# Cross-attention and feed-forward layer on one core: time rows paired before the forward transform, K and Q transformed in eight 64x32 tiles, a float32 inverse transform, and squares for the second layer norm taken by ScalarE

## The chip, the cores and the metric

One core of one Trainium2 chip. The metric is device time in microseconds (us) of one execution. The kernel before takes 1065.87 us, the median of 3 runs (1065.73 to 1066.18).

## What is computed

The input `x` holds 128 sequences of 128 rows (times) by 256 channels, and `ctx_1024` has the same shape. The reference, cut to what matters here:

```python
def reference(x, ctx, wq, wk, wv, wo, W_in, b_in, W_out, b_out):
    q = layernorm(x) @ wq;  k = ctx @ wk;  v = ctx @ wv      # 16 heads of 16
    corr = irfft(rfft(q, time) * conj(rfft(k, time)), n=128) # per channel
    top_vals, top_idx = top_k(corr, 4);  w = softmax(top_vals)
    out = sum_i w[i] * roll(v, top_idx[i] % 16, within the head)
    x = x + out @ wo
    h = quantize_a16(gelu(quantize_a16(layernorm(x)) @ quantize_w8(W_in) + b_in))
    return x + h @ quantize_w8(W_out) + b_out
```

## The kernel before, in words

The work has three stages. The attention stage takes the sequences in 64 pairs and runs them through a software pipeline: step t starts pair t and finishes pairs that were started up to six steps ago. The second stage multiplies the normalized rows by `W_in` (L635), and the third multiplies the quantized hidden values by `W_out` (L666). The change touches the attention stage alone, apart from one scale factor.

Every engine has its own instruction list in program order, and semaphores join them. The order in a list is written by hand: `step(t)` calls the functions of a step, `for t in range(PAIRS - 1)` repeats it, and the last pairs follow as a list of single calls. An engine never passes an instruction that waits.

**TensorE** (`step`, L575) does for pair t the products with `wk` (`project_k`, L464), with `wv` (`project_v`, L515), for pair t-4 with `wo` (`project_out`, L539), for pair t with `wq` (`project_q`, L477), for pair t-3 the weighting of V (`attend`, L527), for pair t the forward transforms of K and Q (`dft_k`, L489, and `dft_q`, L501), and for pair t-1 the inverse transform (`inverse`, L556). The products run in float16 with each operand cut into a high and a low part (three matmuls). The forward transforms are float32, with 128 rows and 64 columns of the array per matmul. The inverse is float16 in three parts, 64 rows by 128 columns. `project_k` and `project_q` write the same bank of PSUM (`bank[1]`), so each waits until the other's result has been taken.

**ScalarE** (`step`, L811) does, in this order: `spread_blocks` of pair t-4 (four copies of 32 partitions each, L756), `take_k` of t-1 (bank 1 to `kf`, through L686), `take_v` of t-1 (L730), `normalize2` of t-6 (second layer norm, L762), `high_ct` of t (high part of the context, L686), `high_cs` of t-2 (high part of the spectrum's product, L686), `exponent` of t-3 (L706), `take_q_scaled` of t-1 (bank 1 times the first layer norm's scale to `qf`, L718), `high_ot`, `high_xt`, `take_ot`, `take_q` (L746 and L747), and in some steps a piece of the weights' quantization.

**VectorE** (`step`, L1309) does: `weigh_hot` of t-4 (L1191), `moments2` of t-6 (L1268), `invert_sum`, `sum_hot`, `mask_sum`, `moments1` of t-1, `spread_weights` of t-4 (L1215), `top_values` of t-3 (four MAX8 on the correlation, L1291), `turn_weights` of t-4 (L1222), `products` of t-2 (L1230 and L1231), `top_places` of t-3, `head_lags`, `statistics1` of t (L1165), `one_hot` of t-3 (L1179), `magnitude` of t-6 (L1274), `residual` of t-5 (L1238), `sum_ex` of t-3, `statistics2` of t-5 (L1245), and in steps 10 to 31 a piece of the weights' scales (L1104, L1109).

**GpSimd** (`step`, L1021) does: `low_ct`, `low_cs` (L1002), `low_xt`, `low_ot` (low parts of the float16 splits), `scale_both` (the reciprocal roots of both layer norms), `add_terms` (L998) and `take_shift`. **SyncE** issues the loads and stores; the load of the next context pair waits for `low_ct` of the one before.

Two waits matter for what follows. `spread_blocks` waits for the transpose of the same pair:

```python
act.wait_ge(S["bt_done"], p + 1)      # in spread_blocks; set by turn_weights (VectorE)
```

and `take_q_scaled`, which frees the transform of Q, runs on ScalarE and waits for nothing of VectorE in its own step except the layer norm's scale.

Of the kernel before, what the change touches and what calls it, by code (L numbers as in the profile page):

```python
# [16 lines left out]
P = 128  # L17
# [4 lines left out]
UNROLL = 10  # L22
# [12 lines left out]
AHEAD = 5  # L35
# [9 lines left out]
C_ALL = C_ROW + 6  # L45
# [8 lines left out]
def by_head(a, axis):  # L54

    s = a.shape
    return a.reshape(s[:axis] + (HD, NH) + s[axis + 1:]).swapaxes(axis, axis + 1).reshape(s)


def constants():  # L60
# [5 lines left out]
    time = t % HD * NH + t // HD  # L66
    angle = 2 * np.pi * np.outer(t, f) / P
    table[:, C_DFT:C_DFT + NF] = np.cos(angle)
    table[:, C_DFT + NF:C_DFT + P] = -np.sin(angle)
    alternating = np.cos(np.pi * t)  # L70
    table[:, C_DFT] = 1 + alternating
    table[:, C_DFT + NF] = 1 - alternating
# [3 lines left out]
    sin[0] = -(1 - alternating) / (4 * P)  # L76
    inverse = np.zeros((P, 2, P))
    for n, m in enumerate((cos, -sin)):
        for b in range(2):
            inverse[b * NF:(b + 1) * NF, n, :] = m * G_UP  # L80
    inv16 = np.zeros((P, 2, 2, P), np.float16)
    inv16[:, 0] = inverse
    inv16[:, 1] = inverse - inv16[:, 0]
    table[:, C_DFT:C_DFT + P] = table[time, C_DFT:C_DFT + P]
# [3 lines left out]
    table[:, C_TURN] = np.where(t % NF == 0, Q_DOWN, -Q_DOWN)  # L88
    for k in range(9):
# [3 lines left out]
    return table.astype(np.float32), inv16  # L93


def xattn_ffn_kernel(nc, x, x_turned, ctx_turned, wq, wk, wv, wo, w_in, b_in, w_out, b_out, table, inv_table, out, x1_dram, h_dram):
# [4 lines left out]
    B, L, D = x.shape  # L101
# [7 lines left out]
    x_v = x.rearrange("(n b) l d -> n l b d", b=2)  # L109
# [4 lines left out]
    with ExitStack() as ctx:  # L114
# [12 lines left out]
        inv16 = sb("inv16", [P, 2, 2, P], F16)  # L127
# [38 lines left out]
        def cut(n, words, shape):  # L166
# [13 lines left out]
        cs16 = cut(1, 512, HALVES)[0].bitcast(F16).rearrange("p s (k e) -> p s k e", k=2)  # L180
# [6 lines left out]
        csum = prod[:, :, 0, :]  # L187
# [17 lines left out]
        half = cut(1, 4, BOTH)[0]  # L205

# [36 lines left out]
            ln2_stats v_done q_done vt_out q_out terms_done sums_done inv_done sc_top hd_done  # L243
            top_done shift_done exp_done mt_out ot_done ot_out ot_low sum_high cs_ready ct_high
# [3 lines left out]
            c_hi_dve c_lo c_f c_out first_int y_inverse bias_chain bias_ready kp_done kf_out k_done w2_done  # L248
# [50 lines left out]
        def _(sp):  # L299
# [12 lines left out]
            def load_turned(p):  # L312
                wait(sp, S["ct_ready"], p)
                sp.dma_start(cturn, ctx_turned[p]).then_inc(s_t_in, 16)
# [14 lines left out]
            def step(t):  # L329
# [10 lines left out]
                if t == 1:  # L340
                    sp.dma_start(inv16[:, :, :, :], inv_table).then_inc(S["direct_in"], 16)
# [91 lines left out]
        def _(pe):  # L433
# [15 lines left out]
            def keep_warm(n, k, table_of=None):  # L449
# [1146 lines left out]
```

## Time and profile before

| what | value |
| --- | --- |
| median of 3 runs | 1065.87 us |
| span of the profiled execution, first to last instruction | 1064.2 us |
| attention stage, to the first matmul of the second stage | 595.2 us |
| TensorE, ScalarE, VectorE, GpSimd busy over the span | 98%, 88%, 91%, 47% |
| granted TensorE clock, mean of the span | 1.000 |

The profile gives no other time of its own execution than the span; 1.7 us of the median lie around it. An instruction's row gives its start and its duration. Neighbours on VectorE and ScalarE overlap by some 0.08 us, so what one of them costs its engine is the distance to the next start, not its duration. Durations in one row of several instructions are those of the merged stretch.

### The profile page before, as it was taken

How to read it: one execution, taken by the hardware profiler on the slowest of the kernel's cores; microseconds unless marked ns; L12 is line 12 of the kernel's file. 1: busy time of each engine (PE TensorE's matmuls, PEld its weight loads, DVE VectorE, ACT ScalarE, POOL GpSimd, SP SyncE). 2: the span in 40 equal slices, each digit the busy share in tenths (PEclk: the TensorE clock that was granted, in tenths of full speed). 3: DMA queues.
4: the chain of work that ended last, by engine and by line, in shares of the span. 5: the costliest groups of instructions: out<-in, count | busy, mean ns of one | idle time of the engine just before them, and what ended most of it. 6: DMA issues, size and time to landing. Idle time of an engine off the chain costs nothing.

```text
span 1064.2 us, 28999 instructions
## 1 busy us (share of the span) xinstructions
PE 1047.4 (98%) x9358; PEld 778.0 (73%) x9358; DVE 965.1 (91%) x2768; ACT 939.9 (88%) x1697; POOL 505.0 (47%) x674
## 2 busy tenths in 40 slices
PE   8999999999999999999998899999999999999998
PEld 6788888888888888888887444444444888888887
DVE  4789999999988888888889999999997999999998
ACT  5888888899999998888888688888888999999996
POOL 5788888888888888888887400000001000000000
PEclk9999999999999999999999999999999999999999
DMA  5454444334445443444431498999999999999995
GB/s 178 130 150 145 121 121 120 121 120 120 121 120 140 121 120 120 121 120 120 120 111 41 132 325 301 300 305 316 309 300 342 356 347 363 355 354 355 346 364 195
DMA packets 141665, 222.59 MB, mean 209 GB/s; under 512 B 72432, under 2 KB 92272, under 8 KB 137456
## 3 DMA queue, kind: packets, MB, share of 16 engines
q1 hardware_dynamic: 140464, 220.12, 62.8%
q8 instruction: 61, 1.00, 0.4%
q10 hardware_dynamic: 1088, 1.05, 0.3%
q14 instruction: 52, 0.43, 0.1%
HBM read 121.00 MB, written 83.89 MB: 193 GB/s over the span
## 4 chain that ended last, share of the span: by engine, by line
PE 94%; ACT 2%; DVE 2%; issue 1%; DMA 1%; POOL 0%; ACTq 0%; DVEq 0%; POOLq 0%
PE sums L666 21%; PE bank L635 10%; PE sums L635 10%; PE sums L464 8%; PE sums L477 8%; PE bank L515 8%; PE sums L539 7%; PE sums L489 6%; PE bank L527 5%; PE bank L501 5%; PE bank L556 5%; PE sums L672 1%; DMA store_x<-in_L_xattn_wv 1%; ACT arena L756 0%; ACT arena L686 0%
## 5 line engine op out<-in xcount | busy, mean ns | idle before, releaser
L666 PE MATMUL sums<-wout,arena 128*128 128x256 f16 x2048 | 229.8, 273 | 1.2 <-DVE arena L1521 1.2
L666 PEld LDWEIGHTS sums<-wout,arena 128*128 128x128 f16 x2048 | 196.9, 98 | 32.5 <-DVE arena L1514 7.3
L1521 DVE SCALAR_TENSOR_TENSOR arena<-arena,wout_rel 128x512 f16<-128x512 int16 x256 | 180.3, 746 | 2.0 <-ACT arena L935 0.9
L756 ACT ACTIVATE arena<-arena 32x128 f32<-32x128 f32 x256 | 78.6, 307 | 47.8 <-DVE arena L1222 45.5
L635 PE MATMUL sums<-arena,win 128*128 128x512 f16 x512 | 115.9, 379 | 1.0 <-DVE arena L1466 0.9
L635 PE MATMUL bank<-arena,win 128*128 128x512 f16 x512 | 115.7, 379 | 0.0
L686 ACT ACTIVATE arena<-arena 128x512 f16<-128x512 f32 x192 | 112.9, 617 | 1.6 <-POOL arena L998 1.1
L1485 DVE TENSOR_REDUCE hmax_all<-arena 128x1 f32<-128x1024 f32 x96 | 111.3, 1211 | 2.9 <-ACT arena L892 2.9
L935 ACT ACTIVATE arena<-arena,wout_rel 128x512 f16<-128x512 int16 x159 | 106.2, 706 | 0.0
L892 ACT ACTIVATE arena<-sums,b_in_sb,z_scale 128x512 f32<-128x512 f32 x128 | 97.4, 778 | 9.8 <-PE sums L635 4.9
L1088 POOL CAST store_x<-one 128x1 bf16<-128x1 f32 x1 | 0.2, 189 | 220.0 <-DVE one L1503 220.0
L928 ACT ACTIVATE arena<-arena,one 128x1536 int16<-128x1536 f32 x63 | 99.2, 1575 | 4.5 <-DVE arena L1521 3.0
L1010 POOL TENSOR_TENSOR arena<-arena 128x512 f16<-128x512 f32 x64 | 74.2, 1159 | 54.8 <-ACT arena L686 54.8
L1291 DVE MAX8 arena<-bank 128x8 f32<-128x128 f32 x256 | 57.1, 286 | 46.9 <-PE bank L556 46.8
L477 PE MATMUL sums<-store_x,arena 128*128 128x256 f16 x768 | 94.3, 273 | 1.0 <-ACT arena L686 0.5
L515 PE MATMUL bank<-arena,store_x 128*128 128x256 f16 x768 | 94.3, 273 | 1.0 <-ACT arena L686 0.6
L635 PEld LDWEIGHTS sums<-arena,win 128*128 128x128 f16 x512 | 50.0, 98 | 61.9 <-issue 1.4
L464 PE MATMUL sums<-store_x,arena 128*128 128x256 f16 x768 | 95.0, 273 | 0.0
L635 PEld LDWEIGHTS bank<-arena,win 128*128 128x128 f16 x512 | 50.1, 98 | 60.4
L539 PE MATMUL sums<-store_x,arena 128*128 128x256 f16 x762 | 93.7, 273 | 0.4 <-POOL arena L1006 0.4
L998 POOL TENSOR_TENSOR arena<-arena 128x512 f32<-128x512 f32 x64 | 81.4, 1272 | 3.5 <-DVE arena L1231 3.4
L477 PEld LDWEIGHTS sums<-store_x,arena 128*128 128x128 f16 x768 | 74.9, 98 | 10.4 <-issue 0.8
(141 smaller groups left out, 2303.7 us busy)
## 6 DMA issues: line engine op xcount, KB each, us to landing
hidden_scratch<-arena SPq DMA_DIRECT2D x32, 1536.0 KB, 5.5
arena<-hidden_scratch SPq DMA_DIRECT2D x64, 768.0 KB, 6.7
arena<-in_ctx_turned SPq DMA_DIRECT2D x64, 256.0 KB, 2.6
arena<-in_x_turned SPq DMA_DIRECT2D x64, 256.0 KB, 2.9
arena<-in_x SPq DMA_DIRECT2D x64, 256.0 KB, 3.7
x_scratch<-arena SPq DMA_DIRECT2D x64, 256.0 KB, 3.4
arena<-x_scratch SPq DMA_DIRECT2D x32, 512.0 KB, 6.0
out<-arena SPq DMA_DIRECT2D x31, 512.0 KB, 4.2
```

Source lines behind the costliest of these rows:

```text
L464: last = nc.tensor.matmul(bank[1][:, b * D:(b + 1) * D], ct16[:, i, c, b * P:(b + 1) * P], w16[:, j, 3, c, :], start=c == 0 and k == 0, st ...
L477: last = nc.tensor.matmul(bank[1][:, b * D:(b + 1) * D], xt16[:, i, c, b * P:(b + 1) * P], w16[:, j, 0, c, :], start=c == 0 and k == 0, st ...
L515: last = nc.tensor.matmul(bank[7][:, e * D:(e + 1) * D], w16[:, j, 1, c, e * P:(e + 1) * P], ct16[:, i, c, :], start=c == 0 and k == 0, st ...
L539: last = nc.tensor.matmul(pair(7)[:, 1, :] if p == PAIRS - 1 and b == 1 else pair(0)[:, b, :], ot16[p % 2][:, i, c, b, :], w16[:, j, 2, c, :],
L635: last = nc.tensor.matmul(bank[f][:, :].rearrange("p (n t) -> p n t", n=4), win16[:, f, c, :], xt[q % 3][:, s, :, c, :], start=s == 0 and ...
L666: last = nc.tensor.matmul(bank[m * 2 + k // 2][:, k % 2 * D:(k % 2 + 1) * D], gbuf[:, s, f, k * P:(k + 1) * P], wout16[:, f, :], start=f = ...
L686: nc.scalar.activation(dst, src, ACT.Copy).then_inc(S[done], 1)
L892: nc.scalar.activation(dst, bank[b][:, :], ACT.Gelu, bias=b_in_sb[:, f:f + 1], scale=z_scale[:, f:f + 1]).then_inc(S[done], 1)
L928: nc.scalar.activation(hq[:, a:b, :].rearrange("p f t -> p (f t)"), src, ACT.Copy, scale=h_up).then_inc(S["c_hq"], 1)
L935: nc.scalar.activation(gbuf[:, 0, f, :], hq[:, f, :], ACT.Copy, scale=wout_rel[:, f:f + 1]).then_inc(S["c_hi_act"], 1)
L1485: V.tensor_reduce(hmax[:, bass.ds(q, 1), k], halls[m][:, 2 * k:2 * k + 2, :], AX_XY, ALU.max, apply_absolute_value=True).then_inc(S["b_max ...
L1521: V.scalar_tensor_tensor(gbuf[:, 1, f, :], hq[:, f, :], wout_rel[:, f:f + 1], gbuf[:, 0, f, :], ALU.mult, ALU.subtract).then_inc(S["c_lo"], 1)
```

## The change

- Host layout: rows t and t+64 of a pair are placed side by side (the inputs are permuted; for the context, the order within the pair is turned around).
- `mix_ct` (new, GpSimd): sum and difference of the context's two halves, before the float16 split. `high_ct` waits for it, and so does the next load of the context.
- `take_q_half` (ScalarE) takes half of Q from the bank with its scale; `mix_q` (new, VectorE) makes the sum and the difference from the bank's other half. They take the place of `take_q_scaled`.
- `transform` takes the place of `dft_k` and `dft_q`: 16 float32 matmuls of 64 rows by 32 columns.
- `inverse` becomes 8 float32 matmuls; `high_cs` and `low_cs` go.
- TensorE's order: `project_q` comes before `project_out`.
- Second layer norm, all but the last five pairs: `residual` in two halves that also give sums, `minus_mean2` (GpSimd), `squares` (ScalarE); `statistics2` and `moments2` go. `normalize2` and `magnitude` move one step later.
- `wo` is loaded in four DMAs and mixed on VectorE once.

```diff
-UNROLL = 10
+UNROLL = 8
-AHEAD = 5
+AHEAD = 6
+BY_BN = 5
+XN_UP = 16.0
...
-            def dft_k(p):
+            def transform(p):
                 if p == 0:
                     pe.wait_ge(S["const_in"], 16)
                 pe.wait_ge(S["kf_out"], p + 1)
                 wait(pe, S["terms_done"], p)
-                for r in range(2):
-                    for b in range(2):
-                        last = nc.tensor.matmul(bank[3][b * NF:(b + 1) * NF, r * D:(r + 1) * D], dft[:, r * NF:(r + 1) * NF], kf[:, b, :],
...
                 pe.wait_ge(S["qf_out"], p + 1)
                 wait(pe, S["q_out"], p)
                 for r in range(2):
+                    for src, dst, turned in ((kf, 3, 1), (qf, 4, 0)):
+                        for b in range(2):
+                            rows = slice((b ^ turned) * NF, (b ^ turned) * NF + NF)
+                            for odd in range(2):
+                                strip = slice((b * 2 + odd) * 32, (b * 2 + odd) * 32 + 32)
+                                last = nc.tensor.matmul(bank[dst][strip, r * D:(r + 1) * D], dft[rows, odd * NF + r * 32:odd * NF + r * 32 + 32], src[rows, odd, :],
+                                                        start=True, stop=True)
+                last.then_inc(S["kq_done"], 1)
...
-                pe.wait_ge(S["cs_ready"], p + 1)
+                pe.wait_ge(S["sums_done"], p + 1)
...
+                        for b in range(2):
+                            half_of = slice(b * NF, (b + 1) * NF)
+                            last = nc.tensor.matmul(bank[5 + b][:, e * P:(e + 1) * P], csum[half_of, k, e * P:(e + 1) * P],
+                                                    inv32[half_of, k, :], start=k == 0, stop=k == 1)
...
             def step(t):                      # TensorE
                 if active(t, 0):
                     project_k(t)
                     project_v(t)
+                    project_q(t)
                 if active(t, 4):
                     project_out(t - 4)
-                if active(t, 0):
-                    project_q(t)
...
-            def take_q_scaled(p):
+            def take_q_half(p):
                 act.wait_ge(S["qp_done"], p + 1)
                 act.wait_ge(S["scales_done"], p + 1)
+                wait(act, S["qf_out"], p)
+                nc.scalar.activation(q_half, pair(1)[:, 1, :], ACT.Copy, scale=rs[(p + AHEAD) % 2][:, 1, 1, :]).then_inc(S["q_half_out"], 1)
...
+            def squares(p):
+                act.wait_ge(S["nm_done"], p + 1)
+                for b in range(2):
+                    last = nc.scalar.activation(xnt[:, p, b, :], x1[p % 2][:, b, :], ACT.Square, bias=nm[p % 2][:, b, :], scale=1.0, accum_out=mv[p % 2][:, 0, b, 1:2])
+                last.then_inc(S["ln2_stats"], 1)
...
-                if active(t, 6):
-                    normalize2(t - 6)
+                if active(t, 7):
+                    normalize2(t - 7)
...
-                if active(t, 2):
-                    high_cs(t - 2)
                 if active(t, 3):
                     exponent(t - 3)
                 if active(t, 1):
-                    take_q_scaled(t - 1)
+                    take_q_half(t - 1)
+                if active(t, 6):
+                    squares(t - 6)
+                if active(t, 0):
+                    high_xt(t)
...
+            def mix_ct(p):
+                pool.wait_ge(s_t_in, p * 16 + 16)
+                wait(pool, S["ct_high"], p)
+                wait(pool, S["ct_ready"], p)
+                nc.gpsimd.tensor_tensor(sd[:, :, 0:P], cturn[:, :, 0:P], cturn[:, :, P:2 * P], ALU.add)
+                nc.gpsimd.tensor_tensor(sd[:, :, P:2 * P], cturn[:, :, 0:P], cturn[:, :, P:2 * P], ALU.subtract).then_inc(S["ct_mixed"], 1)
...
+            def mix_q(p):
+                dve.wait_ge(S["q_half_out"], p + 1)
+                wait(dve, S["kq_done"], p)
+                for k, op in enumerate((ALU.add, ALU.subtract)):
+                    last = V.scalar_tensor_tensor(qf[:, k, :], pair(1)[:, 0, :], rs[(p + AHEAD) % 2][:, 1, 0, :], q_half, ALU.mult, op)
+                last.then_inc(S["qf_out"], 1)
...
+                for b in range(2):            # residual, all but the last five pairs
+                    last = V.scalar_tensor_tensor(x1[p % 2][:, b, :], pair(0)[:, b, :], 1.0 / W_UP, xin[p % UNROLL][:, b, :], ALU.mult, ALU.add,
+                                                  accum_out=mv[p % 2][:, 0, b, 0:1])
+                last.then_inc(S["x1_done"], 1)
...
                 if active(t, 3):
                     top_places(t - 3)
                     head_lags(t - 3)
+                if active(t, 1):
+                    mix_q(t - 1)
                 if active(t, 0):
                     statistics1(t)
                 if active(t, 3):
                     one_hot(t - 3)
-                if active(t, 6):
-                    magnitude(t - 6)
+                if active(t, 7):
+                    magnitude(t - 7)
```

## Rows read from the trace of the kernel before

**Rows 1.** The page: its head and its first part, busy us by engine.

```profile
span 1064.2 us, 28999 instructions
PE 1047.4 (98%) x9358; PEld 778.0 (73%) x9358; DVE 965.1 (91%) x2768; ACT 939.9 (88%) x1697; POOL 505.0 (47%) x674
```

**Rows 2.** Busy us of each engine over twenty steps; then clock, DMA share, GB/s.

```profile
227.80:405.50 177.70, 177.70 (x1921) 146.18 (x1920) 160.33 (x666) 162.96 (x381) 153.14 (x201) 1.00 0.42 122
```

**Rows 3.** Timeline of TensorE over one step: start, us, engine, line, operation.

```profile
305.13 1.48 PE L464 MATMUL sums<-store_x,arena 128*128 128x256 f16 x12
...
307.76 1.47 PE L539 MATMUL sums<-store_x,arena 128*128 128x256 f16 x12
...
310.38 1.06 PE L527 MATMUL bank<-arena,store_x 128*128 128x128 f32 x8
311.37 1.08 PE L489 MATMUL sums<-arena,cst 128*64 128x256 f32 x8
...
313.25 0.84 PE L556 MATMUL bank<-inv,arena 64*128 64x128 f16 x24
314.02 0.28 PE L464 MATMUL sums<-store_x,arena 128*128 128x256 f16 x1
```

**Rows 4.** Timeline of VectorE over the same step.

```profile
305.24 0.89 DVE L1291 MAX8 arena<-bank 128x8 f32<-128x128 f32 x4 [0.85 <-PE bank L556]
306.05 0.29 DVE L1222 STREAM_TRANSPOSE arena<-arena 128x128 f32<-128x128 f32 x1
...
308.71 0.74 DVE L1165 BATCH_NORM_STATS2 arena<-arena 128x6 f32<-128x256 f32 x2
309.37 0.41 DVE L1179 TENSOR_TENSOR sums<-cst,sums 128x256 f32<-128x256 f32 x1
309.90 0.69 DVE L1274 TENSOR_REDUCE xmax<-store_x 128x1 f32<-128x512 f32 x1
310.50 0.68 DVE L1238 SCALAR_TENSOR_TENSOR arena<-sums,arena 128x512 f32<-128x512 f32 x1
...
311.22 0.75 DVE L1245 BATCH_NORM_STATS2 arena<-arena 128x6 f32<-128x256 f32 x2
311.89 0.42 DVE L1191 TENSOR_TENSOR sums<-sums,arena 128x256 f32<-128x256 f32 x1
312.21 0.24 DVE L1268 BATCH_NORM_AGGREGATE arena<-arena 128x2 f32<-128x6 f32 x2
...
313.00 0.29 DVE L1215 TENSOR_TENSOR arena<-arena,sums 128x128 f32<-128x128 f32 x1
```

**Rows 5.** Timeline of ScalarE over the same step.

```profile
306.38 1.26 ACT L756 ACTIVATE arena<-arena 32x128 f32<-32x128 f32 x4 [0.55 <-DVE arena L1222]
307.66 0.60 ACT L686 ACTIVATE arena<-sums 128x512 f32<-128x512 f32 x1
308.16 0.59 ACT L730 ACTIVATE store_x<-bank 128x512 f32<-128x512 f32 x1
308.78 1.09 ACT L762 ACTIVATE store_x<-arena 128x256 f32<-128x256 f32 x2
309.78 1.13 ACT L686 ACTIVATE arena<-arena 128x512 f16<-128x512 f32 x2
...
310.92 0.81 ACT L718 ACTIVATE arena<-sums,arena 128x256 f32<-128x256 f32 x2
```

**Rows 6.** Groups by line and shape: count, busy us, mean ns, idle before and releaser.

```profile
L1254 DVE SCALAR_TENSOR_TENSOR arena<-sums,arena 128x256 f32<-128x256 f32 x1 | 0.4, 425 | 0.0
L1078 POOL TENSOR_TENSOR store_x<-b_out_sb,store_x 128x256 f32<-128x256 f32 x1 | 0.7, 671 | 0.1
L1002 POOL TENSOR_TENSOR arena<-arena 128x512 f16<-128x512 f32 x64 | 74.1, 1158 | 2.4 <-ACT arena L686 2.4
L1104 DVE TENSOR_REDUCE win_max<-store_x 128x1 f32<-128x256 f32 x8 | 3.2, 402 | 0.0
L1109 DVE TENSOR_SCALAR win_max<-win_max 128x8 f32<-128x8 f32 x1 | 0.9, 881 | 0.0
```

More of the change, by code:

```diff
@@ L79, in constants @@
         for b in range(2):
[L80 to L84, printed above, removed]
+            inverse[b * NF:(b + 1) * NF, n, :] = m[by_parity] * G_UP
     table[:, C_ID:C_ID + P] = np.eye(P)
@@ L847, in _ @@
             take_k(PAIRS - 2)
-            normalize2(PAIRS - 7)
+            normalize2(PAIRS - 8)
             exponent(PAIRS - 4)
             high_ct(PAIRS - 1)
+            take_v(PAIRS - 2)
+            take_q_half(PAIRS - 2)
+            squares(PAIRS - 7)
             high_xt(PAIRS - 1)
-            take_q_scaled(PAIRS - 2)
-            high_cs(PAIRS - 3)
-            take_v(PAIRS - 2)
             take_q(PAIRS - 2)
@@ L857, in _ @@
             spread_blocks(PAIRS - 5)
+            take_q_half(PAIRS - 1)
             exponent(PAIRS - 3)
-            take_q_scaled(PAIRS - 1)
+            normalize2(PAIRS - 7)
             high_ot(PAIRS - 5)
-            high_cs(PAIRS - 2)
             take_ot(PAIRS - 5)
             take_q(PAIRS - 1)
+            squares(PAIRS - 6)
             spread_blocks(PAIRS - 4)
             high_ot(PAIRS - 4)
-            high_cs(PAIRS - 1)
             take_ot(PAIRS - 4)
@@ L1023, in step @@
                     low_ct(t - 1)
-                if active(t, 3):
-                    low_cs(t - 3)
+                if active(t, 0) and t > 0:
+                    mix_ct(t)
                 if active(t, 1):
@@ L1038, in _ @@
             low_ct(PAIRS - 2)
-            low_cs(PAIRS - 4)
+            mix_ct(PAIRS - 1)
             low_xt(PAIRS - 2)
-            scale_both(PAIRS - 7)
+            minus_mean2(PAIRS - 7)
+            scale_both(PAIRS - 8)
             take_shift(PAIRS - 4)
@@ L1362, in _ @@
             top_places(PAIRS - 4)
-            magnitude(PAIRS - 7)
+            mix_q(PAIRS - 2)
+            magnitude(PAIRS - 8)
             sum_ex(PAIRS - 4)
@@ L1370, in _ @@
             residual(PAIRS - 6)
-            statistics2(PAIRS - 6)
             invert_sum(PAIRS - 4)
             weigh_hot(PAIRS - 4)
-            moments2(PAIRS - 6)
             sum_hot(PAIRS - 4)
+            top_values(PAIRS - 3)
+            mix_q(PAIRS - 1)
             products(PAIRS - 2)
-            top_values(PAIRS - 3)
             top_places(PAIRS - 3)
```

200 lines of the change are left out of this document (99 added, 101 removed).

## The prediction

> **What bounds the kernel now.** I read the page first: over the whole span TensorE is busy 98%, ScalarE 88%, VectorE 91% [rows 1]. A share over three stages says little about one of them, so I took twenty steps out of the middle of the attention stage: TensorE is busy 177.70 of 177.70 us, which is 8.89 us a step, at a granted clock of 1.00; per step VectorE has 8.02 us of work, ScalarE 8.15 (a few weight pieces among it), GpSimd 7.66 [rows 2]. TensorE sets the pace, and the others have less than 1.3 us a step to spare. The reader should see both: shortening TensorE's list pays at once, and it can't pay much before another engine, or a chain through several, takes over.
>
> Then one step in order of time. On TensorE it runs from 305.13 to 314.02: `project_k` and `project_v` take 2.63 us, the attend 0.99, the two forward transforms 1.88 and the inverse 0.77 [rows 3]. On VectorE the one long idle stretch, 0.85 us, lies ahead of the MAX8, which waits for the inverse; the transpose that follows it ends 0.04 us before ScalarE's four copies start, and those had waited 0.55 us for it [rows 4, 5]. So VectorE and ScalarE are led by TensorE once a step. Today nothing on VectorE waits for ScalarE's later half of the same step, so no circle closes without TensorE.
>
> **TensorE, part by part.** The forward transforms are 8 float32 matmuls of 256 columns in 1.88 us, two side by side (K and Q of either sequence in 64 columns of the array each), with a change of tile shape at the end [rows 3]. That is 0.47 us per pair of matmuls. The new ones are 16 of the same 256 columns, and eight different tiles can run at once. If they do, two rounds cost 4/8 of the streaming now, 0.9 us, and about 0.1 for the change of shape: 1.0. The bounds are 1.0 from below and, if only two run together, twice today's, 3.8; half concurrency gives 1.9. I take 1.0, because two tiles already share the array without loss.
>
> The inverse was 24 float16 matmuls in 0.77 us. Now it is 8 in float32 of 128 columns. The attend has 4 float32 matmuls of 128 columns and full size in 0.99 us [rows 3]; eight half-size ones, two side by side, are the same streaming, so 0.99; if they don't overlap, 1.98. I take 0.99. Together TensorE's list falls from 8.89 to 8.89 - 1.88 - 0.77 + 1.0 + 0.99 = 8.23 us. Moving `project_q` ahead of `project_out` costs TensorE no time of its own, but leaves `take_k` only `project_v` as cover (1.31 us) where it had two products (2.63).
>
> **GpSimd** loses `low_cs` (1.16) and gains `mix_ct`, two float32 additions of 256 columns at 0.67 each (1.34), and `minus_mean2`, a small operation I put at 0.25 [rows 6]: 7.66 + 0.43 = 8.1 us. It stays under what follows. `mix_ct` now releases the context's load, earlier than `low_ct` did, so SyncE's queue is not late.
>
> **ScalarE** loses `high_cs` (0.52) and one of the two halves of `take_q_scaled` (0.36) and gains two squares, at the 0.5 us that `normalize2` takes per half [rows 5] plus a sum's read-out, which no row shows; between 0 and 0.2 each, 0.1 taken. Net +0.3, 8.5 us a step with weight pieces, under 10.
>
> **VectorE** loses `statistics2` (311.22 to 311.89, 0.67) and `moments2` (0.24 less 0.08 of overlap, 0.16). It gains `mix_q`, two operations like L1254's 0.425, so 0.34 apart with the overlap and 0.65 to 0.70 for both [rows 6]. `residual` was 0.60 (0.68 less 0.08) and becomes two halves at 0.34 with a sum each; the sum's read-out has no row, bounds 0 and 0.15 each, 0.05 taken: 0.78. In all 8.02 - 0.67 - 0.16 - 0.60 + 0.65 + 0.78 = 8.0 us.
>
> By sums of work alone, then, every engine would fit in 8.2 to 8.5 us, and the step would shrink. But **the change adds a wait on VectorE**, and I have to name what is queued behind it. `mix_q` of pair t-1 waits for `take_q_half` of pair t-1, which is the seventh call in ScalarE's step. The first call of that same ScalarE step, `spread_blocks`, waits for `turn_weights` of the same VectorE step. And VectorE reaches the next `turn_weights` only after `mix_q` and all that stands behind it. That is a circle of one step, without TensorE in it, and its length is a floor for the step:
>
> - ScalarE, from the first copy to `take_q_scaled`: 306.38 to 310.92, 4.54 us. Out of it go `high_cs` (half of 1.13 for two overlapped copies, 0.52) and the 0.12 that `normalize2` now waits (308.16 + 0.49 to 308.78) [rows 5]. Left 3.90, plus `take_q_half` to its end, 0.45: **4.35**.
> - VectorE, from the place of `mix_q` (just ahead of L1165, 308.71) to L1215 at 313.00: 4.29, plus 0.21 for L1215 itself. Out go 0.67, 0.16, and the 0.20 that L1274 waits (309.37 + 0.33 to 309.90). Left 3.47. MAX8 to transpose 0.81, transpose 0.29 [rows 4]: 4.57. In come `mix_q` 0.65 and 0.18 more for `residual`: **5.40**.
> - Two crossings at the 0.04 us seen between transpose and copies: 0.09.
>
> Sum 9.84 us. VectorE then works 8.0 us and stands 1.8 ahead of `mix_q` in each step. TensorE, with 8.2 us of work, waits for `take_k` (queued behind the copies) ahead of `project_q`.
>
> At this point a page helps to place it. The Trainium skill, TensorEngine Tiling (Array Packing), section PSUM Bottleneck, says that packing speeds up TensorE but not the taking of its results, which may then become the bottleneck. By that rule the change can't keep what its tiles save; by TensorE's sum alone it would.
>
> **The sum.** Full circles run from step 7, where `magnitude` and `normalize2` begin, to about step 61: 54 steps of +0.95, **+51 us**. VectorE's weight pieces stood in its idle time; now they lie on the circle: sixteen of L1104 at 0.402 less 0.08 are 5.1, and six or so short ones, of which the four like L1109 (0.88, 0.80 apart) make up 3.2, come to some 3.7 [rows 6], **+9**. ScalarE's pieces come after `take_q`, in time that it still has: nothing. Filling: `mix_ct` of pair 0 comes ahead of the first split (1.3), and steps 1 to 6 have shorter circles, near 8.2 to 9: **+1.5**. The last pairs: two more `mix_q` round trips and one more small operation of GpSimd for each of the last five, against the shorter inverse chain: **+3**. The second and third stages keep their instructions. Total +64. The profiled execution would go from 1064.2 to 1128, and the median, 1.7 above its span, from 1065.9 to **1130**. The unknown sizes move it so: each 0.1 us on the circle is 5.5 us. `residual`'s sums at 0 give -5, at 0.15 each +11; `mix_q` at 0.80 gives +8. Its own range is 1120 to 1145.
>
> **Rivals.**
>
> *The tiles pay (ends faster).* If ScalarE and VectorE were not held to one another, TensorE's list would be the step: 8.23, 60 steps of -0.66, with +3 for filling and emptying 1066 - 40 + 3 = 1029. For it: the 98% of TensorE, and that no engine has more than 8.5 us of work. Against it: the circle, which needs only that both lists run in order. It decides where the circle is under 8.9, so 0.95 us would have to be missing from it, of which no term but `mix_q` and `residual` is unmeasured. 6%.
>
> *The tiles don't run together.* At 1.9 for the transforms the list is 9.1 and still hidden: about +7 from the first steps, 1137. With 1.98 for the inverse as well it is 10.1, and because MAX8 waits for the inverse and `project_q` for `take_k`, the circle through TensorE (MAX8 0.81, transpose 0.33, copies 1.29, `take_k` 0.60, then `project_q`, `project_out`, attend, transforms, inverse: 7.5) is 10.6 us, some 1174. With two tiles at a time (3.8) it goes beyond 1220. For it: no row shows more than two tiles at once, and each of the eight streams its own data. Against it: two side by side cost nothing. The same page's section Tiling Modes lists 64x32 as eight independent tiles, which is why I don't give this more. 10%.
>
> *The circle is partly cut.* The order of events may let `take_q_half` start earlier than I add up, for example if some of what I counted in series overlaps: a step near 9.3, 1080 to 1115. The step before closes in my terms to 0.05 us, which speaks against it. 6%.
>
> **Chances.** Forecast 78%, tiles partly or not together 10%, partly cut 6%, faster 6%. The range 1110 to 1160 leaves out the fast case and the worst packing. A measurement of this kernel tells 0.2%, 2 us, from no change: faster 0.06, same 0.01, slower 0.93.
>
> **What would show it.** In the changed profile: a step of 9.8 us in the middle of the attention stage; VectorE idle about 1.8 us ahead of `mix_q`, released by ScalarE's copy; MAX8 no longer waiting for the inverse; ScalarE waiting near 2 us for the transpose; TensorE idle about 1.5 us, ahead of `project_q` first of all; the transforms in 1.0 us and the inverse in 1.0. If VectorE's idle time stands ahead of MAX8 again and the step is 8.2 to 8.4, the circle isn't there and I am wrong. If the transform takes over 1.9 us, the packing failed. Steps with weight pieces should be longer by the piece.

## The result, and the profile after

The changed kernel takes **1144.86 us** (median of 4 runs, 1143.14 to 1146.68), the kernel before beside it 1065.8 us. The ratio is **1.0743**, 95% interval 1.0728 to 1.0758: slower by 7.4%, or 79 us. The profiled execution has a span of 1143.1 us, 1.8 under the median; TensorE's granted clock is 0.998 over the span, where it was 1.000; one stretch of the filling is behind that, and it is looked at further below.

The page of the changed kernel, head and first part, answers to [rows 1]:

```profile
span 1143.1 us, 30275 instructions
PE 1024.5 (90%) x9870; PEld 759.9 (66%) x9870; DVE 970.0 (85%) x2838; ACT 942.9 (82%) x1805; POOL 518.1 (45%) x742
```

All busy times hardly moved (TensorE 23 us less, VectorE, ScalarE and GpSimd 3 to 13 us more), but the shares fell. The kernel hasn't more work to do, it waits more. The same stretch as in [rows 2], and one step of it (columns as there):

```profile
227.80:405.50 177.70, 147.89 (x1794) 121.66 (x1792) 140.01 (x602) 144.37 (x367) 135.61 (x191) 1.00 0.35 111
350.28:360.31 10.03, 8.53 (x107) 7.01 (x105) 7.90 (x36) 8.22 (x21) 7.83 (x12) 1.00 0.34 108
```

No engine has more than 8.53 us of work in a step of 10.03 us. Who waits for whom is in the waits of that stretch (engine, line that waited, what ended the wait: us in total, times, longest):

```profile
DVE arena L1250 <- ACT arena L716: 35.5, 17, 2.1
...
ACT arena L748 <- DVE arena L1243: 32.7, 18, 2.0
PE sums L477 <- ACT arena L677: 29.8, 18, 1.8
POOL arena L1021 <- ACT arena L677: 27.3, 17, 1.6
```

L1250 is `mix_q`, L716 `take_q_half`, L748 the four copies of `spread_blocks`, L1243 `turn_weights`. VectorE waits for ScalarE once a step, ScalarE for VectorE once a step, and both for about as long: that is what a circle of two in-order lists looks like. TensorE and GpSimd each wait for ScalarE once a step (GpSimd also 7.7 us in all for VectorE), and nobody waits for them. The timelines of one step; VectorE first, against [rows 4]:

```profile
350.28 0.88 DVE L1326 MAX8 arena<-bank 128x8 f32<-128x128 f32 x4
351.08 0.29 DVE L1243 STREAM_TRANSPOSE arena<-arena 128x128 f32<-128x128 f32 x1
...
355.91 0.88 DVE L1250 SCALAR_TENSOR_TENSOR arena<-sums,arena 128x256 f32<-128x256 f32 x2 [2.09 <-ACT arena L716]
356.71 0.74 DVE L1186 BATCH_NORM_STATS2 arena<-arena 128x6 f32<-128x256 f32 x2
...
358.28 0.42 DVE L1271 SCALAR_TENSOR_TENSOR arena<-sums,arena 128x256 f32<-128x256 f32 x1
358.62 0.08 DVE L1271 DVE_READ_ACCUMULATOR arena<-sums,arena 128x1 f32 x1
358.62 0.42 DVE L1271 SCALAR_TENSOR_TENSOR arena<-sums,arena 128x256 f32<-128x256 f32 x1
...
360.31 0.88 DVE L1326 MAX8 arena<-bank 128x8 f32<-128x128 f32 x4
```

ScalarE, against [rows 5]:

```profile
351.40 1.26 ACT L748 ACTIVATE arena<-arena 32x128 f32<-32x128 f32 x4 [1.69 <-DVE arena L1243]
352.69 0.60 ACT L677 ACTIVATE arena<-sums 128x512 f32<-128x512 f32 x1
353.19 0.59 ACT L722 ACTIVATE store_x<-bank 128x512 f32<-128x512 f32 x1
353.80 1.09 ACT L760 ACTIVATE store_x<-arena 128x256 f32<-128x256 f32 x2
...
355.43 0.45 ACT L716 ACTIVATE arena<-sums,arena 128x256 f32<-128x256 f32 x1
355.79 0.49 ACT L754 ACTIVATE store_x<-arena 128x256 f32<-128x256 f32 x1
356.19 0.19 ACT L754 ACTIVATION_READ_ACCUMULATOR store_x<-arena 128x1 f32 x1
356.28 0.49 ACT L754 ACTIVATE store_x<-arena 128x256 f32<-128x256 f32 x1
```

TensorE, against [rows 3] (the transforms' first and last lines; four pairs of such lines follow one another every 0.2 us):

```profile
353.43 1.47 PE L477 MATMUL sums<-store_x,arena 128*128 128x256 f16 x12 [1.50 <-ACT arena L677]
...
356.05 1.06 PE L521 MATMUL bank<-arena,store_x 128*128 128x128 f32 x8
357.04 0.42 PE L495 MATMUL sums<-arena,cst 64*32 64x256 f32 x4
...
357.74 0.40 PE L495 MATMUL bank<-arena,cst 64*32 64x256 f32 x4
358.07 1.16 PE L550 MATMUL bank<-inv,arena 64*128 64x128 f32 x16
359.17 1.48 PE L464 MATMUL sums<-store_x,arena 128*128 128x256 f16 x12
```

The sixteen transform matmuls take 357.04 to 358.07, 1.03 us, where the eight of the kernel before took 1.88: the eight tiles do run together. TensorE's gain is there, and more than it is lost again ahead of `project_q`, 1.50 us.

Where the 79 us arise is read from the start of `project_k` of some pairs, and of the second stage, in the timelines of TensorE (us):

| | pair 7 | pair 10 | pair 33 | pair 50 | pair 61 | stage 2 |
|---|---|---|---|---|---|---|
| before | 65.0 | 91.7 | 296.2 | 447.4 | 545.2 | 595.2 |
| after | 71.7 | 101.8 | 339.1 | 509.6 | 620.3 | 674.2 |

Filling to pair 7: +6.7. Pairs 7 to 61: +68.4, of which weight pieces 6.6 (pairs 10 to 33 take 237.3 us, 23 steps of 10.03 would be 230.7). The last pairs: +3.9. From there to the end it is 468.9 us against 469.0: stages 2 and 3 are unchanged.

### The profile page after: what moved, and what is told of

It is laid out like the page before. It is cut to its first block and busy times, and to the rows that moved or that the text cites. A ratio compares the mean times of both kernels' runs of the same rounds, so it can differ in the third digit from the quotient of the medians.

```text
span 1143.1 us, 30275 instructions
## 1 busy us (share of the span) xinstructions
PE 1024.5 (90%) x9870; PEld 759.9 (66%) x9870; DVE 970.0 (85%) x2838; ACT 942.9 (82%) x1805; POOL 518.1 (45%) x742
## 5 line engine op out<-in xcount | busy, mean ns | idle before, releaser
L748 ACT ACTIVATE arena<-arena 32x128 f32<-32x128 f32 x256 | 78.5, 307 | 118.5 <-DVE arena L1243 116.2
L1250 DVE SCALAR_TENSOR_TENSOR arena<-sums,arena 128x256 f32<-128x256 f32 x128 | 56.1, 480 | 130.5 <-ACT arena L716 130.5
L477 PEld LDWEIGHTS sums<-store_x,arena 128*128 128x128 f16 x768 | 70.7, 97 | 116.8 <-issue 108.9
L1021 POOL TENSOR_TENSOR arena<-arena 128x512 f16<-128x512 f32 x64 | 74.3, 1160 | 94.6 <-ACT arena L677 94.6
L534 PE MATMUL sums<-store_x,arena 128*128 128x256 f16 x762 | 93.6, 273 | 0.4 <-POOL arena L1017 0.4
L626 PEld LDWEIGHTS sums<-arena,win 128*128 128x128 f16 x512 | 49.9, 98 | 61.6 <-issue 1.2
L509 PEld LDWEIGHTS bank<-arena,store_x 128*128 128x128 f16 x768 | 75.0, 98 | 10.6 <-DVE store_x L1147 1.6
```

What stands on the lines that cost most here:

```text
L477: last = nc.tensor.matmul(bank[1][:, b * D:(b + 1) * D], xt16[:, i, c, b * P:(b + 1) * P], w16[:, j, 0, c, :], start=c == 0 and k == 0, st ...
L509: last = nc.tensor.matmul(bank[7][:, e * D:(e + 1) * D], w16[:, j, 1, c, e * P:(e + 1) * P], ct16[:, i, c, :].rearrange("p (s b j) -> p b ...
L534: last = nc.tensor.matmul(pair(7)[:, 1, :] if p == PAIRS - 1 and b == 1 else pair(0)[:, b, :], ot16[p % 2][:, i, c, b, :], w16[:, j, 2, c, :],
L626: last = nc.tensor.matmul(bank[f][:, :].rearrange("p (n t) -> p n t", n=4), win16[:, f, c, :], xt[q % 3][:, s, :, c, :], start=s == 0 and ...
```

## The experiments

Theory A: the circle of the prediction, with `mix_q` as its closing link, sets the step. All kernels are the changed one with the edit shown. `us` is the device time; "step" is pair 33 to pair 50 over 17, in which no weight piece falls. The kernel before, on the same chips, gave 1066.24, 1065.89, 1065.65 and 1065.8. e7 and e9 to e12 are medians of four or five runs, the others one run each. The device times carry a few us of TensorE's clock: in every trace but those of e5 and of the kernel before there are one to three stretches, 3.4 to 10.2 us each, in the filling or the last pairs, in which the granted clock was 0.50. No stretch of that kind lies between pair 33 and pair 50, so the steps are the surer measure.

| run | us | step | stage 2 starts |
|---|---|---|---|
| changed kernel | 1144.9 | 10.03 | 674.2 |
| e1 project_q after project_out | 1146.1 | 10.03 | 675.3 |
| e2 mix_q late | 1085.5 | 9.03 | 614.8 |
| e3 copy off the circle | 1149.8 | 10.04 | 678.4 |
| e4 copy on the circle | 1174.8 | 10.55 | 703.9 |
| e5 transpose ahead of MAX8 | 1106.4 | 9.37 | 635.6 |
| e6 e2 and e5 | 1075.4 | 8.87 | 604.7 |
| e7 three moves | 1070.4 | 8.75 | 599.6 |
| e8 immediate in mix_q | 1137.7 | 9.92 | 667.0 |
| e9 five moves | 1057.2 | 8.56 | 586.0 |
| e10 e9, wo by SyncE | 1056.5 | 8.53 | 585.8 |
| e11 six moves | **1044.8** | 8.36 | 573.8 |
| e12 e11, bn statistics | 1070.2 | 8.65 | 599.5 |

**e1: is it TensorE's new order?**

```diff
                     project_v(t)
-                    project_q(t)
                 if active(t, 4):
                     project_out(t - 4)
+                if active(t, 0):
+                    project_q(t)
```

> One edit to the changed kernel: TensorE's project_q goes back behind project_out. The changed kernel's step is 10.03 us in the middle of the attention stage and TensorE idles 1.50 us of it ahead of project_q, waiting for ScalarE's copy of K. Theory A (a circle through VectorE and ScalarE, from mix_q to the transpose and from the four copies to take_q_half): TensorE isn't in the circle, so the step stays at 10.0 and the time at 1145 within 3 us; the 1.5 us of idle time only move. Theory B (the reorder is the loss: the copy of K has 1.31 us of cover where it had 2.63): the wait shrinks by most of 1.3 us, the step falls to 8.8 to 9.2 and the time to 1080 to 1095.

1146.1 us, and the step moved by less than 0.01 us. The waits from 296 to 400 us show that TensorE only waits elsewhere now, ahead of the transforms (L495):

```profile
DVE arena L1251 <- ACT arena L717: 20.9, 10, 2.1
...
PE sums L495 <- DVE arena L1251: 12.6, 10, 1.3
```

An engine that is led can have its list put in another order for nothing. The order of TensorE is not the cause.

**e2: `mix_q` behind `magnitude`.** Three operations leave the circle (`statistics1`, `one_hot`, `magnitude`: 356.71 to 358.28 above, 1.57 us), with no work removed.

```diff
-                if active(t, 1):
-                    mix_q(t - 1)
                 if active(t, 0):
                     statistics1(t)
...
                     magnitude(t - 7)
+                if active(t, 1):
+                    mix_q(t - 1)
```

> One edit to the changed kernel: in VectorE's step mix_q moves from ahead of statistics1 to behind magnitude, that is behind 1.6 us of its own work (0.66 + 0.32 + 0.60). Theory A: VectorE did nothing for 2.09 us ahead of mix_q; with 1.6 us of work put there the circle through mix_q is broken up to the rest, and the next floor takes over, the circle through TensorE: MAX8 0.81, transpose 0.33, four copies 1.29, copy of K 0.64, project_q, project_out, attend 3.61, transforms 1.03, inverse 1.15, in all 8.9. Step 8.9 to 9.0, time 1070 to 1078. Theory B (reorder) and theory C (ScalarE's list has become too long by the squares): the order inside VectorE's step changes nothing, step 10.0, time 1145.

1085.5 us: 59 of the 79 us are gone by moving one call. The step, 9.03, is 0.03 above the range that I expected. The time is 7 to 15 us above mine, and that was my arithmetic: 57 steps that are 1.03 to 1.13 shorter take 1144.9 to between 1080 and 1086, not to 1070 to 1078. The step fell by 1.00 and not by the full 1.57 that left the circle, and the waits from 296 to 400 us tell why:

```profile
ACT arena L748 <- DVE arena L1243: 7.7, 12, 0.8
DVE arena L1326 <- PE bank L550: 5.7, 12, 0.6
PE sums L477 <- ACT arena L677: 5.4, 11, 0.5
```

MAX8 waits for the inverse again: a second circle, through TensorE, is the next floor. By the rows of the changed kernel: MAX8 to the copies 1.12, the copies 1.29, `take_k`'s start to `project_q` 0.74, `project_q` and `project_out` 2.62, the attend 0.99, transforms 1.03, inverse 1.10, and some 0.1 back to MAX8: 9.0.

**e3 and e4: the same extra work, off the circle and on it.** One ScalarE copy of 512 columns into a spare buffer, ahead of `squares` (e3) or ahead of the high part of the context (e4).

```diff
+                nc.scalar.activation(spare[:, :], x1[p % 2].rearrange("p b d -> p (b d)"), ACT.Copy)    # e3, in squares
...
+                nc.scalar.activation(spare[:, :], sd.rearrange("p c k -> p (c k)"), ACT.Copy)           # e4, in high_ct
```

> The changed kernel with one more ScalarE copy of 128x512 in each step, 0.52 us, at the start of squares, which is behind take_q_half; its result is not used. Theory A: that place is off the circle, and ScalarE stands idle 1.69 to 2.2 us a step ahead of the four copies, so the step stays 10.0 and the time 1145 within 4 us. Theory C (ScalarE's amount of work sets the pace): +0.52 us for each of some 58 steps, 1175.

> The changed kernel with the same extra copy of 128x512 on ScalarE, 0.52 us, but at the start of high_ct, which stands between the four copies and take_q_half. Theory A: this place is on the circle, so each step grows by all of it, 10.03 to 10.55, and the time by 0.52 x 57, about 30 us, to 1175 (1170 to 1180). Theory C gives the same here, so it is the pair with the run that has the copy off the circle that tells them apart. Theory B: ScalarE's idle time takes it, 1145 to 1150.

The steps are 10.04 and 10.55: nothing off the circle, the full 0.52 us on it. In device time +4.9 and +29.9 us. The 4.9 of e3, a little over the 4 that I allowed, aren't a price of the steps: 0.6 us of them are there at pair 7, 1.0 at pair 61, and 3.2 come between pair 61 and the second stage, where the granted clock was 0.50 for 6.8 us (649.6 to 656.4) as it wasn't in the changed kernel. An attend, a `project_out` and a `project_v` there take 6.65 us for 3.97 in the changed kernel. The last 0.7 lie outside the span. This pair is the sharpest proof of the circle: half a microsecond of the same work costs 0.52 us a step in one place and 0.01 in another place of the same list.

**e5 and e6: the transpose ahead of MAX8, alone and with e2.** `turn_weights` has its data before MAX8 starts, so it can go first, and ScalarE's copies with it.

```diff
-                if active(t, 3):
-                    top_values(t - 3)
                 if active(t, 4):
                     turn_weights(t - 4)
+                if active(t, 3):
+                    top_values(t - 3)
```

> One edit to the changed kernel: in VectorE's step turn_weights (the transpose) goes ahead of top_values (four MAX8, 0.80 us); mix_q stays where it is. Theory A: the circle from mix_q over the transpose to take_q_half loses exactly the MAX8: 10.03 - 0.80 = 9.23 us a step, over 57 steps 46 us less than 1145, that is 1097 to 1103. The four copies then no longer wait behind a MAX8 that waits for the inverse. Were the wait ahead of MAX8 what counts (theory B's form of it, a circle through TensorE), nothing would be won, since no wait ahead of MAX8 is left in the changed kernel: 1145.

> Both edits of VectorE's order: the transpose ahead of MAX8 and mix_q behind magnitude. Theory A: with mix_q late the floor was the circle through TensorE (9.03 a step in that run, 0.8 of it the MAX8); taking MAX8 out of it leaves 8.2, below TensorE's own list of 8.37 (three products and project_out 5.24, attend 0.99, transforms 1.03, inverse 1.10) and near VectorE's 8.0 and GpSimd's 8.1. Step 8.4 to 8.7, 58 steps of -0.33 to -0.63 against the run with mix_q late (1085.5): 1049 to 1067. If some unseen load other than the two circles held the step at 9.0, no gain: 1085.

e5 gives 9.37 a step where the circle less MAX8's 0.80 would be 9.23, and 1106.4 us, 3 above the expectation. e6 shortens both circles and gives 8.87 and 1075.4 us, not the 8.4 to 8.7 and at most 1067 that their lengths promised: a miss, so there had to be a third.

**e7: `take_q_half` ahead of the exponent as well.**

```diff
+                if active(t, 1):
+                    take_q_half(t - 1)
                 if active(t, 3):
                     exponent(t - 3)
-                if active(t, 1):
-                    take_q_half(t - 1)
```

> The two edits of VectorE's order, and on ScalarE take_q_half one call earlier, ahead of exponent (0.11 us and its wait for GpSimd's take_shift). Theory A: it can only help if exponent's wait is on the path to mix_q: step 8.4 to 8.6, time 1045 to 1062, below the kernel before. If TensorE's list is reached already, the same time as with the two edits within 3 us.

1070.4 us, ratio to before 1.0052 (1.0036 to 1.0067), step 8.75. That is 5 us better than e6 and again short of what I expected (8.4 to 8.6 a step, at most 1062 us). Its waits from 296 to 400 us:

```profile
ACT store_x L722 <- PE bank L509: 4.5, 12, 0.5
PE sums L495 <- DVE arena L1250: 3.7, 12, 0.8
DVE arena L1250 <- ACT arena L716: 2.3, 12, 0.2
```

Read from top to bottom this is the third circle: ScalarE's `take_v` (L722) waits for `project_v`, `mix_q` waits for ScalarE, the transforms wait for `mix_q`. With the spacings of the rows it is `take_v` 0.62, normalizations 1.0, high copies 0.52, `take_q_half` 0.45, `mix_q` 0.88, transforms 1.03, inverse 1.10, `project_k` and `project_v` 2.62, and the hand-over from `mix_q`'s end to the transforms 0.25: 8.47. Two more hand-overs, 0.14 from `project_v` to `take_v` and 0.04 from `take_q_half` to `mix_q`, make it 8.65. The mean of 17 steps is 8.75.

**e8: the price of `mix_q`.** The second operand is a number in place of a scale per row, so this kernel leaves out the scale of one half of Q.

```diff
-V.scalar_tensor_tensor(qf[:, k, :], pair(1)[:, 0, :], rs[(p + AHEAD) % 2][:, 1, 0, :], q_half, ALU.mult, op)
+V.scalar_tensor_tensor(qf[:, k, :], pair(1)[:, 0, :], 1.0, q_half, ALU.mult, op)
```

> The changed kernel with mix_q's per-partition scale replaced by the number 1.0 (the scale of this half of Q is left out). In the changed kernel the two operations of mix_q start 0.40 us apart, and residual's, of the same size with a constant and a sum, 0.34. Theory: the scale read from memory is the 0.06 us. Then the circle loses 0.12 us, the step is 9.91 and the time 7 us less, 1138. If the 0.06 comes of something else (the operands' places), no change: 1145 within 3 us.

1137.7 us. The lines' own view, of the changed kernel and then of this one (ns: least, median, most):

```profile
L1250 DVE SCALAR_TENSOR_TENSOR arena<-sums,arena x128: 473/480/488, 16.0 to 642.7; 128x256 f32<-128x256 f32 x128
```

```profile
L1250 DVE SCALAR_TENSOR_TENSOR arena<-sums,arena x128: 414/420/426, 14.8 to 634.0; 128x256 f32<-128x256 f32 x128
```

A scale read from memory costs 0.06 us an operation, 0.12 a step on the circle, 7 us of device time.

**e9: V read later, GpSimd's scales earlier.** On top of e7:

```diff
                     take_k(t - 1)
-                    take_v(t - 1)
...
                     high_ct(t)
...
+                if active(t, 1):
+                    take_v(t - 1)
                 if active(t, 1):
                     take_q_half(t - 1)
...
-                if active(t, 5):
-                    low_ot(t - 5)
                 if active(t, 6):
                     minus_mean2(t - 6)
                 scale_both(t - 7)
+                if active(t, 5):
+                    low_ot(t - 5)
```

> All of the three moves before, and two more: ScalarE reads V out of PSUM (take_v) only after the first normalizations and the high parts of C, and GpSimd computes the scales of layer norm 2 (scale_both) ahead of the low parts of the weighted V. Nothing is left out. Theory A (what sets the step with three moves is a circle of 8.7 us: project_v's end, take_v 0.62, the normalizations 1.0, the high copies 0.52, take_q_half 0.45, mix_q 0.88, a crossing 0.25, the transforms 1.03, the inverse 1.10, then the projections of K and V): with take_v off it, the circle is 0.6 us shorter, and TensorE's own list, 8.3 to 8.4 us, takes over: pair 33 to pair 50 at 8.35 to 8.5 us a step against 8.74, stage 2 from about 580, device time 1048 to 1058 us. Rival C (the step of 8.74 us is VectorE's or ScalarE's own sum, and no order changes it): 1068 to 1072 us.

1057.2 us, ratio 0.9926 (0.9909 to 0.9943): the first version ahead of the kernel before, by 0.7%. The time is in my range, the step, 8.56, a little above it. The waits from 296 to 400 us, then one hand-over in the timeline of GpSimd and in that of SyncE's queue, name the reason:

```profile
POOL arena L1013 <- DMA arena<-in_ctx_turned: 7.6, 10, 1.9
...
PEld sums L534 <- POOL arena L1018: 2.8, 4, 1.1
```

```profile
338.31 1.16 POOL L1026 TENSOR_TENSOR arena<-arena 128x512 f16<-128x512 f32 x1
```

```profile
339.49 0.33 SPq L318 DMA_DIRECT2D arena<-in_x_turned  x1
...
340.82 0.48 SPq L314 DMA_DIRECT2D arena<-in_ctx_turned  x1
```

The context's buffer is free at 338.3, when `mix_ct` is done, but its load is the fourth in SyncE's queue, behind one that waits for `low_xt` (L1026) and two more. It is issued at 340.8, GpSimd starts late with it, and `project_out` (L534) waits for GpSimd.

**e10: is the filling slow by the load of wo?** In the changed kernel ScalarE's queue issues four transfers of wo for 2.69 us in the first step. Here SyncE issues them one step later, and what uses them follows.

```diff
 # SyncE, t == 1
+                    load_wo()
...
 # ScalarE
-                if t == 0:
-                    load_wo()
-                if t == 1:
+                if t == 2:
                     high_w(2)
...
 # VectorE
-                if t == 1:
+                if t == 2:
                     mix_wo()
                     low_w(2, 3)
```

> As the run before it, and the four transfers that bring wo in for its two halves are issued by SyncE one step later in place of ScalarE, with the mix of wo and its split a step later too. Nothing is left out. Theory A (the filling lost some 5 us of its 6.7 because these issues held 2.69 us of ScalarE's queue at 10.55 us, ahead of take_k of pair 0): pair 10 starts 3 to 5 us earlier than in the run before it, and so does everything behind; 1044 to 1054 us. Rival (the filling is slow since each first step is a circle of its own, and the issues only happened beside it): no change, within 1 us.

1056.5 us, within 1 us of e9, and pair 10 even starts 2.0 us later (99.1 against 97.1). By its number the rival holds: this move buys nothing. But the run doesn't clear the issues. TensorE's wait ahead of the first `project_q` fell from 2.54 to 0.77 us, as the theory wants, and yet the first transforms start only 0.47 us earlier (17.10 against 17.57). VectorE's timeline shows what else stands there once `mix_q` is late: it is behind `statistics1`, and that waits for the load of x of the next pair:

```profile
15.43 0.75 DVE L1186 BATCH_NORM_STATS2 arena<-arena 128x6 f32<-128x256 f32 x2 [2.82 <-DMA arena<-in_x]
...
25.36 0.75 DVE L1186 BATCH_NORM_STATS2 arena<-arena 128x6 f32<-128x256 f32 x2 [3.86 <-DMA arena<-in_x]
```

The first of these waits is in e9 too (4.07 us). The second is not: with the wo issues in SyncE's queue, the context's load behind them goes out at 16.12 in place of 12.76, and the next load of x at 22.44 in place of 20.26. The move took one wait away and made another. What the issues cost in the changed kernel, where `mix_q` stands ahead of `statistics1`, no run shows.

**e11: the context's load first.** On top of e9, in SyncE's step:

```diff
-                if active(t, 0) and t > 0:
+                if active(t, 0) and 0 < t <= 5:
                     load_turned(t)
+                if t >= 5:
+                    load_turned(t + 1)
                 if active(t, 0) and t > 0:
                     load_x_turned(t)
```

> The five moves before, and a sixth on SyncE's queue: from pair 5 on, the load of the transposed context rows of the next pair is issued as soon as GpSimd has mixed the last ones, ahead of the load of the transposed rows of x, which waits for their low parts. Nothing is left out. Theory D (with five moves GpSimd has become part of the circle: it waited 7.6 us in 104 for this transfer, which stood 1.3 us behind the end of the low parts in SyncE's queue, and TensorE's project_out then waited for the low parts of the weighted V, 4.3 us in the same stretch): both waits go or shrink, pair 33 to pair 50 at 8.36 to 8.48 us a step against 8.56, device time 1048 to 1054 us. Rival E (8.56 us is already TensorE's own list, 102 us busy in 104): within 1.5 us of 1057.2 us.

**1044.8 us** (1044.26 to 1045.47), ratio 0.9804 (0.9788 to 0.982), 3 us below my range. Six moves with no work removed turn 7.4% slower into 2.0% faster. Busy time of the engines from 296 to 400 us, and then the longest waits that are left there:

```profile
296.00:400.00 104.00, 104.00 (x1285) 87.90 (x1284) 99.87 (x425) 101.94 (x260) 97.23 (x138) 1.00 0.46 136
```

```profile
PEld bank L551 <- issue: 4.9, 12, 0.4
DVE arena L1328 <- PE bank L551: 3.3, 12, 0.3
...
```

TensorE is busy for all of the 104 us, and the step is its list again, 8.36 us in place of 8.89. This version beats both kernels.

**e12: what does the layer norm part bring there?** e11 with the second layer norm's sums taken back to `bn_stats` and `bn_aggr`:

```diff
-BY_BN = 5
+BY_BN = 64
...
 # ScalarE
-                    squares(t - 6)
...
 # GpSimd
-                    minus_mean2(t - 6)
...
 # VectorE
+                    moments2(t - 6)
...
+                    statistics2(t - 5)
```

> The kernel of the run before it, with the layer norm part of the change undone alone: the residual no longer sums its rows, ScalarE's squares and GpSimd's mean are gone, and VectorE computes the statistics of layer norm 2 with bn_stats and bn_aggr as before the change. Nothing is left out. Theory F (with its idle time gone VectorE is close to the limit, so the layer norm part carries its own weight): VectorE's list, some 8.1 us without its waits, gets 0.67 + 0.16 us longer and sets the step at 8.9 to 9.0 us, device time 1072 to 1082 us. Rival G (ScalarE is the closer one, 98.5 us busy in 104, and loses 1 us a step by this): no change or faster, at most 1 us above the run before it.

1070.2 us, 25.5 above e11. From 296 to 400 us:

```profile
296.00:400.00 104.00, 102.52 (x1252) 84.92 (x1251) 103.07 (x423) 90.10 (x206) 96.00 (x144) 1.00 0.44 129
```

VectorE is busy for 103.07 of 104 us: theory F. The step, 8.65, is below my 8.9, and the time 2 us below my range; but with VectorE full, its weight pieces cost too: pairs 10 to 33 take 208.9 us, 9.08 a step. Without this part of the change the faster transforms would bring nothing, even in the order of e11 (ratio to before 1.0043, 1.0026 to 1.0059).

## Why the prediction was right, and where its terms were off

The forecast was 1130 us with a range of 1110 to 1160 and 93% for slower; measured 1144.86. The mechanism stands: e2, e3 with e4, and e5 each move the step as a circle does, and e1 rules out TensorE's order. Of the 15 us by which the forecast is low, some 10 are the circle's length, 5 the filling, 1 the last pairs, and the weight pieces give 2 back. By its own steps:

- **The circle, 9.84 us.** Measured 10.03: ScalarE's part 4.48 for 4.35 (351.40 to 355.88), VectorE's 5.49 for 5.40, crossings 0.06 for 0.09. ScalarE's 0.13 is the 0.12 that I took out ahead of `normalize2` as a wait: it is there still (353.19 to 353.80 with nothing to wait for). On VectorE `mix_q` takes 0.80 to the next start, not 0.65, of which 0.12 are its scale's coming from memory (e8); L1254 [rows 6], which I priced it by, has 0.425. This outweighs `residual`, 0.69 for 0.78.
- **54 steps, +51 us.** It was +61.8 (68.4 less 6.6); 54 × 1.14 are 61.6. The 0.19 us of the circle makes the 10 us.
- **Weight pieces, +9.** 6.6, the steps of pairs 10 to 31 being 10.1 to 10.5 us long, as the forecast says that they should. The sixteen reductions cost what I gave them (0.33 to the next start, 5.2 in all). The seven short ones between 184 and 319 us cost 1.3 in all, not 3.7: the four that I priced at 0.80 by L1109 are 0.25 to 0.27 from their next one here, though their lines of the kernel are the same. Why they are shorter is open.
- **Filling, +1.5.** This is the term that was off by most for its size: +6.7. The 1.3 that I gave `mix_ct` isn't there at all: `project_k` of pair 0 starts at 7.22, before at 7.42. The steps that follow I had at 8.2 to 9, and from pair 1 on they are 8.6 to 9.1, but I set them against a full step of 8.89, and the kernel before fills faster than that: from pair 0 to pair 4 its steps are 7.25, 8.23, 7.14 and 8.29, where these are 10.88, 8.99, 8.92 and 8.61. TensorE's timeline of the first steps, then ScalarE's:

```profile
14.03 1.47 PE L477 MATMUL sums<-store_x,arena 128*128 128x256 f16 x12 [2.58 <-ACT arena L677]
17.07 0.42 PE L495 MATMUL sums<-arena,cst 64*32 64x256 f32 x4 [1.57 <-DVE arena L1250]
24.37 0.42 PE L495 MATMUL sums<-arena,cst 64*32 64x256 f32 x4 [1.96 <-DVE arena L1250]
33.88 0.42 PE L495 MATMUL sums<-arena,cst 64*32 64x256 f32 x4 [1.68 <-DVE arena L1250]
...
42.49 0.42 PE L495 MATMUL sums<-arena,cst 64*32 64x256 f32 x4 [0.78 <-DVE arena L1250]
```

```profile
10.55 2.69 ACTq L690 DMA_DIRECT2D store_x<-in_L_xattn_wo  x4
13.29 0.60 ACT L677 ACTIVATE arena<-sums 128x512 f32<-128x512 f32 x1 [2.11 <-issue]
```

  In the kernel before, the longest wait ahead of the transform of Q in these pairs is this one, in pair 1:

```profile
21.11 1.08 PE L501 MATMUL bank<-arena,cst 128*64 128x256 f32 x8 [1.32 <-ACT arena L718]
```

  Three things are in these rows. In the first three pairs nothing stands between `project_q` and the transforms, in the fourth only the attend, to cover the way through ScalarE and now VectorE too: 6.0 us of waits ahead of L495, where the kernel before had 1.55 ahead of its transform of Q. `project_q` of pair 0 waits 2.58 us for `take_k`, where before it waited 0.50, and ScalarE stood idle for 2.11 of them while it issued the loads of wo; e10 doesn't settle what they cost. And TensorE's clock dropped for a while, columns as in [rows 2]:

```profile
25.80:29.20 3.40, 3.40 (x25) 2.56 (x24) 2.00 (x7) 0.72 (x2) 2.72 (x5) 0.50 0.01 2
```

  In that stretch the inverse of pair 0 takes 1.69 us and `project_k` of pair 2 takes 2.33, where they take 1.10 and 1.32 at a clock of 1.00: 1.6 us. That the longer way is the largest part is read from these rows, and no run took it away; in e11 pair 7 still starts 4.6 us later than before, with 6.8 us at a clock of 0.50 by then.
- **The last pairs, +3.** It was 3.9.
- **TensorE's list, 8.23.** The rows have 1.03 for the transforms (1.0) and 1.10 for the inverse (0.99): 8.37 with these, and e11 runs at 8.36.
- **The other engines.** In the step shown VectorE has 7.90 us (8.0), ScalarE 8.22 (8.5), GpSimd 7.83 (8.1).
- **The idle times.** VectorE 2.09 ahead of `mix_q` (1.8), ScalarE 1.69 for the transpose (near 2), TensorE 1.50 ahead of `project_q` (1.5), and MAX8 follows with no wait.
- **The page on packing.** The Trainium skill, TensorEngine Tiling (Array Packing), section PSUM Bottleneck: packing doesn't speed up the taking of results. The runs agree only in part. The change got slower, but not because the taking became longer: in e11 the same readers and the same tiles fit in 8.36 us. It was where they stand in the lists. The section Tiling Modes of the same page of the Trainium skill, with eight independent 64x32 tiles, is borne out by the 1.03 us.

The rival "tiles pay" gave 1029 us if no circle held the engines. It was wrong for the change as made, and right for its pieces: e11 reaches 1044.8, with steps of 8.36 for 8.23 and 4.6 and 3.1 us more than before in filling and last pairs, where I had allowed 3 in all. Of the 3.1, 1.7 are two groups of products at a granted clock of 0.50 (548.3 to 551.7). "Tiles don't run together" is dead by the 1.03 us. "Partly cut" is dead for the changed kernel, and describes e2 and e5.

## What to carry to other kernels

When a change adds a wait between two engines that both run a fixed list, add up the circle: from the new wait back to itself through both lists, with everything that stands in between; busy shares don't show it. Once it is known, moving one call past work that nobody on the circle needs can be worth more than making an operation faster (here 59 us for the place of `mix_q`, 7 us for its 0.12), and after every such cut the next circle, or a queue of DMA issues, has to be looked for anew.

## What the runs showed of the hardware beyond that

- Eight float32 tiles of 64 rows by 32 columns run side by side: 16 matmuls of 256 columns in 1.03 us, where 8 in tiles of 128x64 took 1.88.
- VectorE's SCALAR_TENSOR_TENSOR on 256 columns from PSUM takes 480 ns with a scale from memory and 420 ns with an immediate one (e8).
- TensorE's granted clock fell to 0.50, the lower of its two levels (1.2 GHz), where its list had gaps: in the changed kernel at 25.8 us, after 10 us in which it was busy for 6.7, and then not again before 1141.9. That stretch of 3.4 us cost 1.6 us. The four runs of this kernel took 1143.14 us at a mean clock of 1.000, 1144.86 (twice) at 0.998 and 1146.68 at 0.995: that such stretches make the difference fits, but one trace alone was kept.
- Reading a sum out costs VectorE no spacing (the halves of `residual` start 0.34 us apart), but costs ScalarE 0.09 us (ACTIVATE at 355.79, read-out at 356.19, the next ACTIVATE at 356.28).
- From the end of `mix_q` to the transforms that wait for it 0.25 us pass (335.06 to 335.31 in e7), where VectorE and ScalarE hand over in 0.03.
